# The global attention row joins the residual by an accumulating transfer

## The reference

```python
h = layernorm(x) * (1 + ca) + sa                       # x: 4 x 2048 x 512, float32
Q, K, V = h @ Wq.T + bq, h @ Wk.T + bk, h @ Wv.T + bv   # in 64 segments of 128 rows
local = softmax(Q @ K.T * SCALE) @ V                    # inside a segment
summ = first row of each segment of h
global_out = softmax(Qg @ Kg.T * SCALE) @ Vg            # 16 segments of a batch, from summ
x = x + ga * ((local + global_out[segment]) @ Wo.T + bo)   # one global row for 128 tokens
h = layernorm(x) * (1 + cb) + sb
x = x + gb * experts(h)      # route by argmax; first 512 tokens of an expert are kept
```

## Time and profile before

| | us |
|---|---|
| median of 3 runs | 1865.91 (1865.58 to 1867.16) |
| the profiled execution | 1863.25 |
| its span, first to last instruction | 1861.6 |
| PE busy | 1787.6 (96%) |
| DVE busy | 1170.0 (63%) |
| ACT busy | 828.2 (44%) |
| POOL busy | 803.4 (43%) |
| mean granted PE clock | 0.987 of full speed |

### The profile page before, as it was taken

One profiled execution on the slowest core, in us unless ns is written; L12 is line 12 of the kernel. 1 busy time (PEld: TensorE's weight loads), 2 busy tenths in 40 slices (PEclk: granted clock), 3 DMA queues, 4 the chain that ended last, 5 costly groups with the idle time before them and its releaser, 6 DMA issues.

```text
span 1861.6 us, 28129 instructions
## 1 busy us (share of the span) xinstructions
PE 1787.6 (96%) x9125; PEld 1486.2 (80%) x9142; DVE 1170.0 (63%) x1879; ACT 828.2 (44%) x1323; POOL 803.4 (43%) x664
## 2 busy tenths in 40 slices
PE   8999999999999469999999999998998999999998
PEld 3688888888888358889888888887888888888886
DVE  4577788788787653546545454548648796455862
ACT  2544544554554332334434233346446464334542
POOL 2134455445443421424444241426547766233632
PEclk9999999999999789999999999999999999999999
DMA  8444654654663634443543434345454555434622
GB/s 282 145 133 132 187 136 126 191 135 124 193 180 115 158 114 145 137 163 130 182 156 130 147 134 171 117 144 182 159 185 166 201 198 184 144 118 164 220 82 68
DMA packets 146362, 287.54 MB, mean 154 GB/s; under 512 B 17889, under 2 KB 18477, under 8 KB 146310
## 3 DMA queue, kind: packets, MB, share of 16 engines
q1 hardware_dynamic: 115338, 221.27, 34.0%
q0 software_dynamic: 30976, 65.64, 13.9%
HBM read 237.71 MB, written 67.49 MB: 164 GB/s over the span
## 4 chain that ended last, share of the span: by engine, by line
PE 91%; DVE 2%; issue 2%; ACT 2%; POOL 1%; DMA 1%; POOLq 0%; DVEq 0%; ACTq 0%; SPq 0%
PE bank L332 27%; PE bank L334 26%; PE bank L333 26%; PE bank L781 3%; PE bank L723 2%; PE bank L601 1%; PE bank L824 1%; PE bank L590 1%; PE bank L539 1%; PE bank L773 1%; PE bank L753 1%; POOL yo L1675 0%; DMA out_dram<-yo,tok_x 0%; DVE h_lo L1451 0%; PE bank L734 0%
## 5 line engine op out<-in xcount | busy, mean ns | idle before, releaser
L1451 DVE TENSOR_TENSOR h_lo<-h_f,h_hi 128x512 fp32r<-128x512 f32 x256 | 220.3, 882 | 356.4 <-ACT h_f L1100 356.2
L1099 ACT ACTIVATE h_hi<-bank,b_col 128x512 fp32r<-128x512 f32 x256 | 176.4, 689 | 594.1 <-PE bank L334 579.6
L332 PE MATMUL bank<-bt_hi,w_hi 128*128 128x512 f32 (+4 forms) x1024 | 359.7, 351 | 9.0 <-DVE w_lo L1422 4.4
L333 PE MATMUL bank<-bt_lo,w_hi 128*128 128x512 f32 (+4 forms) x1024 | 358.5, 350 | 0.0
L334 PE MATMUL bank<-bt_hi,w_lo 128*128 128x512 f32 (+4 forms) x1024 | 358.4, 350 | 0.0
L332 PE MATMUL bank<-w_hi,h_hi 128*128 128x512 f32 x832 | 326.6, 393 | 1.0 <-issue 0.8
L333 PE MATMUL bank<-w_lo,h_hi 128*128 128x512 f32 x832 | 324.8, 390 | 0.0
L334 PE MATMUL bank<-w_hi,h_lo 128*128 128x512 f32 x832 | 324.7, 390 | 0.0
L332 PEld LDWEIGHTS bank<-bt_hi,w_hi 128*128 128x128 f32 x1024 | 193.4, 189 | 35.1 <-issue 9.4
L333 PEld LDWEIGHTS bank<-bt_lo,w_hi 128*128 128x128 f32 x1024 | 193.5, 189 | 20.8
L334 PEld LDWEIGHTS bank<-bt_hi,w_lo 128*128 128x128 f32 x1024 | 193.5, 189 | 20.1
(11 more groups left out here) (266 smaller groups left out, 3130.4 us busy)
## 6 DMA issues: line engine op xcount, KB each, us to landing
raw<-in_L_ffn_W_dram SPq DMA_DIRECT2D x128, 1024.0 KB, 7.0
xa<-in_L_attn_x_dram SPq DMA_DIRECT2D x16, 1024.0 KB, 5.4
xr<-in_L_attn_x_dram SPq DMA_DIRECT2D x16, 1024.0 KB, 8.3
h_rows<-sb_tab SPq DMA_DIRECT2D x16, 1024.0 KB, 10.3
out_dram<-xr SPq DMA_DIRECT2D x16, 1024.0 KB, 12.1
h_rows<-h POOLq DMA_DIRECT2D x16, 1024.0 KB, 9.5
b_bc<-in_L_ffn_b_dram SPq DMA_DIRECT2D x16, 256.0 KB, 6.2
wm_a<-in_L_wmod_dram SPq DMA_DIRECT2D x2, 1024.0 KB, 10.6
```

What stands on the lines that cost most here:

```text
L332: pe.matmul(o, a_hi, b_hi, start=start, stop=False)
L333: pe.matmul(o, a_hi, b_lo, start=False, stop=False)
L1099: act.activation(h1_hi[b % 2][:, j, :], h_bank[j][:, :], ACT.Relu, bias=bias)
L1451: dve.tensor_tensor(h1_lo[b % 2][:, j, :], h1_f[:, j, :], h1_hi[b % 2][:, j, :].bitcast(F32), ALU.subtract) \
```

## The change

The global row no longer passes through PE. In the prologue it is multiplied by the gate `ga` (a new small product GAROW spreads `ga` over the segments, ACT copies it, one DVE product makes `g_ga`) and stored in float32. In the stage POOL adds the four rows of a group, broadcast over the 128 partitions, to xr in SBUF by an accumulating transfer of 1 MB, at the head of its next iteration and for group 0 as soon as the rows are stored. DVE waits for it (`xr_summed`) before line 1391, where it waited for xr's load. The row product, its selector, the grows loads and their waits are gone. On DVE `route_slots` moves in front of the split of the probabilities, two query rows stay behind that split, and the other two, with the query constant, go behind the third u_lo. The diff, cut to its core:

```diff
-    global_dram = nc.dram_tensor("global_rows", (NSEG * 3, D), BF16, kind="Internal").ap()
+    global_dram = nc.dram_tensor("global_rows", (NSEG, D), F32, kind="Internal").ap()
-    seg_sel = keep("seg_sel", [P, GS, P], BF16)
-    grows = [keep(f"grows{i}", [P, D], BF16) for i in range(2)]
+    seg_batch = keep("seg_batch", [NBATCH, NSEG], F32)
...
@@ sync
-        sp.wait_ge(g_split_done, 1)
-        sp.dma_start(global_dram.rearrange("(n t) d -> n t d", t=3), g_split[:]).then_inc(g_stored, 16)
+        sp.wait_ge(g_gated, 1)
+        sp.dma_start(global_dram, g_ga[:]).then_inc(g_stored, 16)
...
-                wait_past(sp, av_full, 4 * i.n - 4)
-                sp.dma_start(grows[i.par][0:3 * GS, :], global_dram[bass.ds(i.n * 3 * GS, 3 * GS), :]) \
-                    .then_inc(grows_in[i.par], 16)
@@ tensor
         product(PGT, pe.transpose(pro_bank(PGT)[:, 0:NSEG], pg[:], ident[0:NSEG, 0:NSEG]))
+
+        pe.wait_ge(mod_fixed, 2)
+        pe.wait_ge(made, POOL_MADE)
+        bank_free(GAROW)
+        product(GAROW, pe.matmul(pro_bank(GAROW)[0:NSEG, :], seg_batch[:], modr[:, GA, :], start=True, stop=True))
...
-                pe.wait_ge(grows_in[p1.par], 16 * (p1.half + 1))
...
-                    split3(pe, big[s][:, :], pt_hi[:, s, :], pt_lo[:, s, :], u_hi[:, s, :], u_lo[:, s, :], True, False)
-                    pe.matmul(big[s][:, :], seg_sel[:, s, :], grows[p1.par][:], start=False, stop=True) \
+                    split3(pe, big[s][:, :], pt_hi[:, s, :], pt_lo[:, s, :], u_hi[:, s, :], u_lo[:, s, :], True, True) \
                         .then_inc(av_full, 1)
@@ scalar
+        copy_out(GAROW, g_b[:], pro_bank(GAROW)[0:NSEG, :])
@@ vector
-        dve.tensor_copy(g_split[:, 0, :], g_a[:]).then_inc(gsum_step, 1)
-        dve.wait_ge(gsum_step, 8)
-        dve.tensor_tensor(g_x[:], g_a[:], g_split[:, 0, :], ALU.subtract).then_inc(gsum_step, 1)
-        dve.wait_ge(gsum_step, 9)
-        dve.tensor_copy(g_split[:, 1, :], g_x[:]).then_inc(gsum_step, 1)
-        dve.wait_ge(gsum_step, 10)
-        dve.tensor_tensor(g_split[:, 2, :], g_x[:], g_split[:, 1, :], ALU.subtract).then_inc(g_split_done, 1)
+        dve.tensor_tensor(g_ga[:], g_a[:], g_b[:], ALU.mult).then_inc(g_gated, 1)
...
-            if cur:
-
-                for s in range(GS - 1):
-                    query_row(i, s)
+            if prev3 and cur:
+                route_slots(p3)
             if prev:
                 dve.wait_ge(pt_hi_done, p1.n + 1)
                 dve.tensor_tensor(pt_lo[:].rearrange("p s t -> p (s t)"), pt_bank[:, :],
                                   pt_hi[:].rearrange("p s t -> p (s t)").bitcast(F32), ALU.subtract).then_inc(pt_split, 1)
-            if prev3:
+            if prev3 and not cur:
                 route_slots(p3)
+            if cur:
+
+                for s in range(2):
+                    query_row(i, s)
...
-                dve.wait_ge(xr_in[p1.par], 16 * (p1.half + 1))
+                dve.wait_ge(xr_summed[p1.par], 16 * (p1.half + 1))
...
-                query_row(i, GS - 1)
...
-                    if s == 0:
+                    if s == 2:
+                        query_row(i, 2)
+                        query_row(i, 3)
                         query_const(i)
@@ gpsimd
+        def add_global(g):
+
+            pool.wait_ge(xr_in[g.par], 16 * (g.half + 1))
+            stand_alone(pool, pool_passed)
+            part = global_dram[bass.ds(g.n * GS, GS), :].unsqueeze(0).to_broadcast([P, GS, D])
+            pool.dma_start(xr[g.par][:], part, accum_op=ALU.add).then_inc(xr_summed[g.par], 16)
+
         def iteration(i, prev, nxt, prev3):
             p1 = i.plus(-1)
             b = batch_of(p1)
+            if prev:
+                if isinstance(i.n, int) and i.n == 1:
+                    pool.wait_ge(g_stored, 16)
+                add_global(p1)
             if nxt:
                 normalise1(i.plus(1))
```

More of the change, by code:

```diff
@@ L201, in build_block @@
                                       ("bqk", [NBATCH, 2, D], F32), ("hg_t", [P, KC, NSEG], F32))
-    g_split, brow, u_row, gg_t = over(r_tab + 8 * KB, ("g_split", [NSEG, 3, D], BF16), ("brow", [P, D], F32),
+    g_ga, brow, u_row, gg_t = over(r_tab + 8 * KB, ("g_ga", [NSEG, D], F32), ("brow", [P, D], F32),
                                       ("u_row", [1, D], F32), ("gg_t", [P, KC, NSEG], F32))
@@ L264, in build_block @@
     gsum_masked, gsum_negb, gsum_exp, gsum_prob = (sem(f"gsum_{k}") for k in ("masked", "negb", "exp", "prob"))
-    g_split_done, g_stored, table_cleared = sem("g_split_done"), sem("g_stored"), sem("table_cleared")
+    g_gated, g_stored, table_cleared = (sem(k) for k in ("g_gated", "g_stored", "table_cleared"))
     x_in = [sem(f"x_in{i}") for i in range(2)]
     xr_in = [sem(f"xr_in{i}") for i in range(2)]
-    grows_in = [sem(f"grows_in{i}") for i in range(2)]
+    xr_summed = [sem(f"xr_summed{i}") for i in range(2)]
     ln1_step, ln1_ready, ln1_rstd, xn_done = (sem(k) for k in ("ln1_step", "ln1_ready", "ln1_rstd", "xn_done"))
@@ L334, in split3 @@
         return pe.matmul(o, a_lo, b_hi, start=False, stop=stop)
-    (MCH, SCT, BCOL, FIRST4, WOT, UCOL, MCOL, VCH, HGT, LATE4, GROWS, GGT, SG, BROW, SCOL, PGT, TG,
-     B1T, PRO_END) = (0, 4, 5, 6, 7, 11, 12, 13, 17, 18, 19, 20, 21, 22, 23, 24, 25, 26, 27)
+    (MCH, SCT, BCOL, FIRST4, WOT, UCOL, MCOL, VCH, HGT, LATE4, GROWS, GGT, SG, BROW, SCOL, PGT,
+     GAROW, TG, B1T, PRO_END) = (0, 4, 5, 6, 7, 11, 12, 13, 17, 18, 19, 20, 21, 22, 23, 24, 25, 26, 27, 28)
     def pro_bank(q):
@@ L350, in build_block @@
     POOL_MADE = 9
-    DVE_MADE = 9
+    DVE_MADE = 7
     def results_done(eng, e, b):
@@ L1286, in query_const @@
                 .then_inc(qc_ready, 1)
-        dve.wait_ge(g_split_done, 1)
         tok4 = [P, GS, E]
@@ L1548, in _ @@
         pool.memset(ones[:], 1.0).then_inc(made, 1)
-        pool.memset(seg_sel[:], 1.0).then_inc(made, 1)
+        pool.memset(seg_batch[:], 1.0).then_inc(made, 1)
         pool.wait_ge(made, 3)
@@ L1553, in _ @@
                            channel_multiplier=-1).then_inc(made, 1)
-        pool.affine_select(out=seg_sel[:], in_=seg_sel[:], compare_op=ALU.is_ge, fill=0.0, base=0,
-                           pattern=[[-3, GS], [0, P]], channel_multiplier=1).then_inc(made, 1)
+        spb = NSEG // NBATCH
+        pool.affine_select(out=seg_batch[:], in_=seg_batch[:], compare_op=ALU.is_ge, fill=0.0, base=0,
+                           pattern=[[1, NSEG]], channel_multiplier=-spb).then_inc(made, 1)
         pool.wait_ge(made, 5)
-        pool.affine_select(out=seg_sel[:], in_=seg_sel[:], compare_op=ALU.is_ge, fill=0.0, base=2,
-                           pattern=[[3, GS], [0, P]], channel_multiplier=-1).then_inc(made, 1)
+        pool.affine_select(out=seg_batch[:], in_=seg_batch[:], compare_op=ALU.is_ge, fill=0.0, base=spb - 1,
+                           pattern=[[-1, NSEG]], channel_multiplier=spb).then_inc(made, 1)
         pool.iota(tokids[:], pattern=[[P, NSEG]], base=0, channel_multiplier=1).then_inc(made, 1)
```

2 lines of the change are left out of this document (removed).

## The result

The changed kernel takes 1945.45 us, median of 4 runs (1941.02 to 1947.69), against 1866.13 for the kernel before: a ratio of 1.0422, 95% interval 1.0409 to 1.0436. It is slower, as forecast, but by 79 us and not by 52: 1945.45 is 1.45 us above the range. The profiled execution has a span of 1945.6 us against 1861.6, 84.0 us more.

The account below looks back on a forecast made before the run. PE, 91% of the chain, bounds the kernel; -1.9 (prologue) + 35.2 (twelve intervals) + 7.5 (last two) + 11.5 (tail) = +52.3 us on 1863.25 gives 1915.6, median 1918 us; range 1871 to 1944 (8 in 10).

Parts of the forecast that it names:

- rival A: Attention stage: the accumulating transfer's landing sets the period, 1918 us in all, own range 1893 to 1937; chance 0.62.
- DVE's new order: Slots before the probabilities' split, query rows 2 and 3 later: no cost to PE by itself, 0.7 us of cover.
- Rival B: The transfer into xr runs like a plain load, 2.65 us; period 34.95 us, 1874.5 us in all; chance 0.17.
- Rival C: Transfer lands before U + 33.3 (U: PE starts a value product), PE sets pace: 1851 to 1859 us; chance 0.12.
- xr's own load: Attention stage: second of SP's four transfers, data in near +19, POOL asks at +22, so no second wait.
- Rival D: POOL's queue refuses the second accumulate's descriptors while the first runs: +43 us on rival A, 1961; chance 0.09.
- The step that failed: Loop's end: after the stall DVE runs 0.8 us later, but the third u_lo waits for ACT until +9.2, so no lengthening.
- The chain behind the release: From SP's release, U + 11.6, through four megabytes and two accumulates to U + 37.8; PE waits 3.7 us per iteration.
- The tail: After U(15): the new transfer, behind h2's accumulate and beside weight loads, makes DVE begin 11.5 us late.
- The last two intervals: Group 14's xr load waits for group 12's output store, and the last has no x load: estimated +7.5 us.
- The expert stage: Expert stage, not touched by the change: 0 us.
- The prologue: Prologue and first iteration, to U(1): shorter DVE split work and PE's idle 1.08 us gone, -1.9 us.

Follow-up runs that it names:

- the plain copy: The changed kernel with the transfer into xr overwriting xr instead of accumulating; only the attention stage can be read: intervals of 34.98 us against 39.15.
- the early query rows: The changed kernel with all four query rows ahead of DVE's wait for the summed residual: 1904.81 us, ratio 1.0205, interval 36.16.
- the order alone: The kernel before with DVE's new order only, row product still on PE and no accumulating transfer: 1872.7 us, ratio 1.0031.
- the gap filled: The changed kernel with twelve needless products on PE where it would idle, in each of 15 iterations: 1924.33 us, ratio 1.0309, interval 37.80.
- transfer alone: The changed kernel with DVE's old order, the accumulating transfer kept: 1907.83 us, ratio 1.0223, interval 36.54.
- the transfer ahead with the old order: The changed kernel with the accumulate into xr issued ahead of h2's, at the end of its own iteration, and DVE's old order: 1857.41 us, ratio 0.9949.
- no transfer: The changed kernel without the accumulating transfer, DVE waiting for xr's load, global row left out of the result: 1853.64 us, ratio 0.9929.
- half width: The changed kernel with the accumulating transfer adding only 256 of 512 columns; only the attention stage is read: interval 35.44 us against 39.15.

## Why the prediction was right in sign and short in size

**What held.** The mechanism is rival A's: DVE waits for the transfer into xr, PE for DVE, once per interval. PE's own 34.1 us (measured 34.08 without the transfer), 5.5 us for the accumulate (the mean of the two that ran alone), and the price of the other edits (12.9 us gained, predicted some 15) are right or near. DVE's new order was put at nothing by itself and costs 6 us.

Rival B describes the plain copy (34.98), and not this transfer. Rival C's condition, accumulates under 4.7 us, was missed narrowly (4.9 from landing to landing), but behind h2's the full accumulate into xr never landed before U + 34.1, and C needed + 33.3 (its own sum, -15 and 4 to 8 in the tail, gives 1855 to 1859 us, not 1851). xr's own load, said to be no second wait, lands at U + 20.5 in the turns from U(11) and U(12) and at + 22.7 to + 24.5 in the nine slow ones, where it holds up POOL's issue (+ 23.5 to + 25.2); xr's sum still lands 4.9 us behind h2's, so nothing of this shows in the interval. Rival D is refuted by the rows of the early query rows: the second accumulate was issued 1.2 us behind the first, and the engines ran on without a break at 188 GB/s. The Trainium skill's fit for a transfer issued by GpSimd (DMA: Bandwidth & Descriptors, Anatomy of one DMA), 4.4 us for 1 MB, doesn't describe an accumulate: with empty engines the one of h2 had a median of 9.6 us to landing and the one into xr behind it 13.6.

**The step that failed** is the last one of the chain: "What follows the stall on DVE is some 0.8 us later relative to U than today, but the third u_lo waits for ACT until +9.2 anyway, so the loop does not get longer by it." It treats what follows U as running at the old pace. Behind a gap of 3.26 us PE does not. The granted clock falls from full (2.4 GHz) to half (1.2 GHz) for a while, and the first products of the value product come 0.43 us apart. So ACT's u_hi, the third u_lo (ended at U + 11.2, not + 9.9), the query rows, SP's release (+ 13.7, not + 11.6) and both accumulates shift, and the next gap is as long again: the loop feeds the delay back to itself. Of the 2.1 us by which the release is late, 1.3 are the clock and 0.9 the slow query row. The query row is a term of its own: it was put at 0.74 us and took 1.65 here, and query rows are slow in the order alone too, where the clock stays at full speed in every turn.

Two comparisons show the price. In the kernel after itself, the intervals from U(11) and U(12), where the clock stays up, take 36.5 us and the nine behind a drop 39.1 to 40.8; the one from U(1), where the clock stays up but the query row is slow (release at + 12.3), takes 38.0. With the gap filled, the clock is kept in all twelve intervals, and they take 450.7 us: the prediction said 453.6, and the kernel after took 468.1, which is the excess of 49.7 - 35.2 = 14.5 us. The release is then at + 11.4 to + 11.7 in six of the twelve (in the turn shown above both late query rows are clear of POOL's products, 0.68 and 0.69 us) and at + 12.1 to + 12.5 in the others.

Two agreements are luck in part. The chain behind the release was sized 1 us too long: near the release that the prediction names, the interval is 36.5 to 37.0 us in seven of eight turns and not 37.8, since h2's sum lands at + 30.7 and not + 31.5, and xr's 4.9 us behind it and not 5.5. This hid a part of what the clock cost. And the idle time, 49.9 us against 14 x 3.7 = 52, comes out near because gaps of 3.0 to 4.7 us at the end of the slow turns and of 2.2 us at the end of those from U(11) and U(12) are averaged.

**Why order and transfer cost more together.** The old order releases SP at U + 8.8, the new one at + 13.7. While DVE waits for xr's load only, little of it shows (35.11 against 34.89). With two accumulates behind the plain megabytes it does, but not evenly. Medians of the intervals that begin at U(2) to U(12), in us:

| SP's release | xr's sum lands | interval | where |
|---|---|---|---|
| U - 2.9 to - 0.9 | U + 35.0 | 35.8 | early query rows, 11 turns |
| U + 8.8 | U + 35.3 | 36.2 | transfer alone, 11 turns |
| U + 11.4 to + 11.7 | U + 35.6 | 36.9 | filled gap 6, kernel after 2 |
| U + 12.3 to + 12.5 | U + 36.9 | 37.8 | filled gap, 5 turns |
| U + 13.7 to + 15.0 | U + 38.5 | 39.3 | kernel after, 9 turns |

The kernels differ in more than the release, but the picture is plain: up to about + 11.5 a later release costs little, and behind that nearly all of it comes back in the interval. The new order alone ends beyond this point (+ 12.5), and the low clock takes it further and delays POOL's issues as well (h2's at + 21.6 to + 23.0, not + 20.5). The early query rows take the interval from 39.15 to 36.16 by that edit alone.

**The tail** was mis-sized by 2.2 us. DVE's rows of group 15 come at U(15) + 38.85 with 13.17 us of idle time before them; the new transfer stands behind h2's and beside four weight loads. Issued ahead of h2's, and with the old order, it leaves 25.05 us, the value of before (25.12). Of the 13.7 us, 1.1 are DVE's order, as the kernel without the transfer has 26.20.

**The last two intervals** cost 9.95 us and not 7.5. The mechanism is the one named: the load of xr for group 14 waits for the output's store of group 12 and is issued at U(13) + 30.5, in the kernel before at + 22.8. (SP's last x load is that of iteration 13, so the groups without one are the last two, and not the last three.)

**The expert stage** was put at nothing and took 7.8 us more. Its first 10 us ran at 0.53 against 0.81, with 29 matmuls done instead of 40. But the clock at the opening doesn't order the kernels: the order alone opened at 0.53 and took 1199.0 us for the stage, the transfer ahead with the old order opened at 0.83 and took 1201.5. The five other kernels that compute the whole took 1198.3 to 1202.4. So a part of the 7.8 us is there in each of these kernels (one profiled execution each, 1196.0 in the kernel before), and what makes it stays open.

**The prologue** was predicted 1.9 us shorter and came 2.7 longer. U(1) falls into two groups, 104.5 to 104.8 (no transfer, half width, ahead with the old order, and the filled gap once the 2.7 us of its filler are taken off its 107.55) and 107.1 to 108.7 (all others of the changed kernels, and the order alone at 108.1, whose prologue is that of before). In the slow group PE lags by 1.5 to 3.1 us at the end of the first 50 us: from 30 to 50 us the clock is 0.83 in the kernel after and 0.91 in the kernel without the transfer, whose prologues are the same. The saving of 1.6 us is there where the start is the fast one. A further 1.0 us is PE's wait for the transfer at U(1). What sets the start was not tried, and each kernel's start is known from one profiled execution.

## What to carry to other kernels

When a wait is added in front of the bounding engine, price its gap twice: the idle time, and the slower products behind it; then follow both once around the loop to the release that starts the late transfer. If the queue holds two transfers and only one of them has a reader soon, issue that one first: here this turned +4.2% into -0.4% without moving a byte less. The margin that it leaves is then worth a look: with the new order of DVE it was 1 us. Edits of order that are free while a transfer is early stop being free once it is late, so their costs can't be added from separate measurements.

## What the runs showed of the hardware

- An accumulate of 1 MB costs the DMA engines 5.5 us into HBM, and the pair of one into HBM and one into SBUF 11 us, so the same again (188 GB/s with the engines full); the second lands 4.9 us behind the first. A plain copy into the same tile from the same rows lands 2.5 us behind it and shortens the interval by 4.2 us. Behind h2's accumulate, with empty engines before both, the landing comes 13.6 us after the issue.
- Gaps of 1.32 us (early query rows) and 1.93 us (transfer alone) on PE left the products behind them starting 0.23 to 0.24 us apart after the first; the gap of 3.26 us was followed by starts 0.43 us apart. The length of the gap alone doesn't tell: gaps of 1.79 us (transfer alone, U(12)) and 2.15 us (kernel after, U(13)) were followed by 0.43 us as well, and gaps of 2.93 us (early query rows, U(2)) and 3.28 us (kernel after, U(11)) were not. Over the intervals of the kernel after, the low clock took 22.8 us of PE time.
- DVE's query rows, two inputs of 128x512 in SBUF, took 689 ns in the kernel before, whose order keeps them clear of POOL's wide tensor operations, and 1087 on average in the kernel after; the constant of 4 columns took 1049 ns, and 0.22 us in the kernel before. In the listed turn POOL's row products run beside both. The Trainium skill (SBUF — State Buffer, SBUF: two separate sides) says that a VectorE operation with two SBUF inputs and a GpSimd operation that reads SBUF lock each other out for a whole instruction. The trace agrees for the query rows beside POOL's wide operations: 1.65 us beside its products at 397.88, 0.69 when clear of them. Beside POOL's products of 4 columns (line 1571 in the kernel before) 61 of the 64 query rows run, and still take 0.69 us. By name and count, kernel after and then kernel before:

```profile
L1270 DVE SCALAR_TENSOR_TENSOR qc_junk<-xa,vc_tab 128x512 f32<-128x512 f32 x56 | 60.9, 1087 | 1.0
L1277 DVE TENSOR_SCALAR per_tok<-per_tok,qc_bc 128x4 f32<-128x4 f32 x14 | 14.7, 1049 | 1.4 <-DVE qc_junk L1270 0.6
```

```profile
L1278 DVE SCALAR_TENSOR_TENSOR qc_junk<-xa,vc_tab 128x512 f32<-128x512 f32 x56 | 38.6, 689 | 1.1
```
